# A four-layer graph network in one kernel: the mirrored attention sums leave PSUM through ScalarE and are added in SBUF on GpSimd

## The reference, cut to what matters

```python
h = relu(layernorm(x));  x = x + L0(h, adj)      # (A @ (h @ W + b)) / column degrees
h = relu(layernorm(x));  x = x + L1(h, adj)      # normalised adjacency @ (h @ W), relu
h = relu(layernorm(x));  x = x + L2(h, adj)      # attention, below
h = relu(layernorm(x));  x = x + L3(h, adj)      # hypergraph product with adj

def L2(x, adj, weight, bias):
    h = x @ weight
    h_norm = h / maximum(norm(h, axis=1), 1e-8)
    sim = h_norm @ h_norm.T                       # symmetric
    attn = softmax(sim + log(adj + 1e-8), axis=1) # = (adj + 1e-8) * exp(sim), over its row sum
    return attn @ h + bias
```

## Time and profile before

| what | us |
|---|---|
| median of 3 runs | 1335.18 |
| lowest, highest run | 1329.08, 1477.92 |
| the profiled execution | 1339.48 |
| its span, first to last instruction | 1337.7 |
| attention, first scores to last mirrored product, about | 570 to 1129 |

### The profile page before, as it was taken

The page is one execution under the profiler, slowest core; times in us unless marked ns, Lnnn a source line. Parts: engine busy times, 40 slices in busy tenths (PEclk is TensorE's granted clock), DMA queues, the critical chain, the costliest instruction groups (busy, mean ns, idle before and its releaser), DMA issues.

```text
span 1337.7 us, 26725 instructions
## 1 busy us (share of the span) xinstructions
PE 1271.8 (95%) x9548; PEld 944.0 (71%) x9548; DVE 1012.4 (76%) x2273; ACT 629.6 (47%) x1480; POOL 365.2 (27%) x422
## 2 busy tenths in 40 slices
PE   6999999979999999989999999999999977899998
PEld 4788788854455555557776777777767655688887
DVE  7878789899455555579888978978889988776642
ACT  5654456546223222266656755656656654311111
POOL 2000000012422223213223332332333222465433
PEclk9999999999999999999999999999999999999999
DMA  9999999932111220125653554544544414250500
GB/s 225 247 340 294 307 354 380 382 145 84 48 57 54 63 64 17 48 87 157 198 174 119 174 163 126 173 133 148 177 122 155 135 56 119 79 150 26 150 25 25
DMA packets 122899, 199.93 MB, mean 149 GB/s; under 512 B 13201, under 2 KB 83857, under 8 KB 122769
## 3 DMA queue, kind: packets, MB, share of 16 engines
q1 hardware_dynamic: 115568, 194.04, 47.0%
q10 hardware_dynamic: 7200, 4.20, 1.1%
HBM read 147.85 MB, written 50.33 MB: 148 GB/s over the span
## 4 chain that ended last, share of the span: by engine, by line
PE 55%; issue 13%; DVE 11%; DMA 5%; POOL 4%; ACT 2%; SPq 1%; ACTq 0%; DVEq 0%; POOLq 0%
PE ps L1823 12%; PE ps L1619 8%; PE ps L1620 8%; PE ps L1732 7%; DMA acc<-in_adj 5%; PE ps L1717 5%; PE ps L1718 5%; DVE ring L795 4%; POOL ring L693 3%; PE ps L1784 3%; PE ps L1749 2%; DVE small L807 2%; SPq L431 1%; DVE ring L1043 1%; DVE ring L1073 1%
## 5 line engine op out<-in xcount | busy, mean ns | idle before, releaser
L693 POOL TENSOR_TENSOR ring<-ring 128x512 f16<-128x512 f32 (+3 forms) x133 | 151.9, 1149 | 327.8 <-ACT ring L1493 327.8
L1581 PE MATMUL ps<-val_hi,ring 128*128 128x257 f16 x1024 | 227.2, 274 | 5.0 <-DVE ring L795 5.0
L1582 PE MATMUL ps<-val_lo,ring 128*128 128x256 f16 x1024 | 227.1, 274 | 0.0
L1619 PE MATMUL ps<-ring,acc 128*128 128x512 fp8e4 x512 | 196.7, 384 | 6.7 <-DVE acc L933 6.7
L1732 PE MATMUL ps<-hnt 128*128 128x512 f16 (+3 forms) x864 | 196.3, 363 | 1.0 <-DVE ring L1043 1.0
L1620 PE MATMUL ps<-ring,acc 128*128 128x512 fp8e4 x512 | 196.6, 384 | 0.0
L795 DVE STREAM_TRANSPOSE ring<-acc 128x1024 uint8<-128x1024 uint8 x128 | 151.2, 1219 | 39.1 <-DMA acc<-in_adj 39.0
L1717 PE MATMUL ps<-val_hi,ring 128*128 128x257 f16 x490 | 134.7, 275 | 22.8 <-POOL ring L693 13.9
L1372 ACT ACTIVATE hnt<-ring 128x512 bf16<-128x512 uint8 (+1 forms) x192 | 115.1, 602 | 82.7 <-DVE ring L795 82.7
L1717 PE MATMUL ps<-val_hi,hs 128*128 128x257 f16 x534 | 145.8, 273 | 1.1 <-DVE acc L1106 0.6
L1749 PE MATMUL ps<-val_hi,hs 128*128 128x257 f16 x534 | 145.8, 273 | 0.0
(11 more groups left out here) (234 smaller groups left out, 2371.3 us busy)
## 6 DMA issues: line engine op xcount, KB each, us to landing
acc<-in_adj SPq DMA_DIRECT2D x256, 256.0 KB, 9.3
turned_dram<-ring SPq DMA_DIRECT2D x56, 512.0 KB, 2.9
ring<-turned_dram SPq DMA_DIRECT2D x224, 128.0 KB, 2.9
at_dram<-ring SPq DMA_DIRECT2D x32, 512.0 KB, 9.8
ring<-at_dram SPq DMA_DIRECT2D x64, 256.0 KB, 3.9
ring<-at_dram SPq DMA_DIRECT2D x24, 512.0 KB, 3.8
ring<-at_dram SPq DMA_DIRECT2D x9, 1024.0 KB, 9.7
xs<-in_x SPq DMA_DIRECT2D x12, 256.0 KB, 10.6
```

Of the source, the lines that this page charges most:

```text
L693: nc.gpsimd.tensor_tensor(lo2[m % 2][:, k:GW], p2t[m % 2][:, k:GW], hi2[m % 2][:, k:GW], ALU.subtract).then_inc(sem["lo2_done"], 1)
L1581: nc.tensor.matmul(ps[:, k % 8, 0:D + 1], lhs, val_hi0[:, t, 0:D + 1], start=(t == 0), stop=False)
L1582: last = nc.tensor.matmul(ps[:, k % 8, 0:D], lhs, val_lo0[:, t, :], start=False, stop=(t == NB - 1))
L1619: nc.tensor.matmul(ps[:, bank + c, :], g_hi[:, t, c * P:(c + 1) * P], src, start=(t == 0), stop=False)
```

## The change

The mirrored sum is copied from PSUM by ACT. In group 0 the copy goes straight to the row in `acc`; in later groups it goes to one of two rows of 257 in SBUF (`mirrored`, laid over the bias row and an unused part of the weights), and GpSimd adds it to `acc`. ACT does the copy right behind weights_high, GpSimd the addition ahead of mirror_low. PE's waits for a free bank, and the last layer's first wait, go by the new semaphore acc_copied; acc_added now counts only the 84 additions on GpSimd, and the group sums of DVE and the reuse of a `mirrored` row wait for it. Products, precision and DMAs are as before.

```diff
@@ -35,7 +35,7 @@
...
-s_done exp_raw exp_done turned written p1_done hi1_done lo1_done pv1_done t_done p2_done hi2_done lo2_done pv2_done acc_added
+s_done exp_raw exp_done turned written p1_done hi1_done lo1_done pv1_done t_done p2_done hi2_done lo2_done pv2_done acc_copied acc_added
...
@@ -125,8 +125,8 @@
         p2t = [temps[:, (2 + i) * 1024:(3 + i) * 1024].bitcast(F32) for i in range(2)]
         hi2 = [temps[:, 4096 + i * 512:4608 + i * 512].bitcast(F16) for i in range(2)]
         lo2 = [temps[:, 5120 + i * 512:5632 + i * 512].bitcast(F16) for i in range(2)]
-        w_all = sb("w_all", [P, 3 * C * D], F32)
-        w = w_all[:, :].rearrange("p (l c d) -> p l c d", l=3, c=C)
+        w_all = sb("w_all", [P, 3 * C * D + 1], F32)
+        w = w_all[:, 0:3 * C * D].rearrange("p (l c d) -> p l c d", l=3, c=C)
         w1_hi = w_all[:, 0:256].bitcast(F16).rearrange("p (c d) -> p c d", c=C)
         w1_lo = w_all[:, 256:512].bitcast(F16).rearrange("p (c d) -> p c d", c=C)
         w2_hi = w_all[:, 512:768].bitcast(F16).rearrange("p (c d) -> p c d", c=C)
@@ -134,9 +134,10 @@
         e_t = [ring[:, 6 * N + i * 1024:6 * N + (i + 1) * 1024].bitcast(F32) for i in range(2)]
         turned = [ring[:, a:a + 2048].bitcast(F32) for a in (N + 2048, 6 * N + 2048)]
         back = [ring[:, a:a + 2048].bitcast(F32) for a in (7 * N + 2048, 7 * N)]
-        misc = sb("misc", [P, 3 * D], F32)
+        misc = sb("misc", [P, 3 * D + 1], F32)
         xn = [misc[:, i * D:(i + 1) * D] for i in range(2)]
         bias_bc = misc[:, 2 * D:3 * D]
+        mirrored = [misc[:, 2 * D:3 * D + 1], w_all[:, 5 * D:6 * D + 1]]
         hs = sb("hs", [P, 4 * D], F32)
         ht = [hs[:, i * D:(i + 1) * D] for i in range(2)]
         s32 = [hs[:, (2 + i) * D:(3 + i) * D] for i in range(2)]
@@ -693,6 +694,13 @@
                 nc.gpsimd.tensor_tensor(lo2[m % 2][:, k:GW], p2t[m % 2][:, k:GW], hi2[m % 2][:, k:GW],
                                         ALU.subtract).then_inc(sem["lo2_done"], 1)
 
+            def add_mirror(n):
+
+                (g, j), m = order[n], n_outer[n]
+                pool.wait_ge(sem["acc_copied"], m + 1)
+                since(pool, sem["acc_added"], m - NB + (g + 1) * GB - n_outer[opens[1]])
+                nc.gpsimd.tensor_tensor(acc[:, j, :], acc[:, j, :], mirrored[m % 2], ALU.add).then_inc(sem["acc_added"], 1)
+
             for n in range(NS):
                 if n - 1 in late_at["project1"]:
                     add_bias(late_at["project1"][n - 1])
@@ -700,11 +708,17 @@
                     root_var2(late_at["project1"][n])
                 if n in late_at["project2"]:
                     root_norm(late_at["project2"][n])
+                for o in mirrors_at(n - 1):
+                    if outer[o] and order[o][0] > 0:
+                        add_mirror(o)
                 for o in mirrors_at(n + 1):
                     mirror_low(o)
                 for g, i in tail_at(n):
                     if i == 9:
                         root_var3(g)
+            for o in mirrors_at(NS - 1):
+                if outer[o]:
+                    add_mirror(o)
             root_var3(NG - 2)
             root_var3(NG - 1)
             for n in range(NB // 2):
@@ -1083,16 +1097,6 @@
                                                    ps[:, 6, b0 * P:GW].rearrange("p (b i) -> p b i", i=P),
                                                    ALU.add, ALU.mult).then_inc(sem["p2_done"], 1)
 
-            def add_mirror(n):
-
-                (g, j), m = order[n], n_outer[n]
-                dve.wait_ge(sem["pv2_done"], place[n] + 1)
-                if g == 0:
-                    nc.vector.tensor_copy(acc[:, j, :], ps[:, mirror_bank(n), 0:D + 1]).then_inc(sem["acc_added"], 1)
-                else:
-                    dve.wait_ge(sem["acc_added"], m - NB + (g + 1) * GB)
-                    nc.vector.tensor_tensor(acc[:, j, :], acc[:, j, :], ps[:, mirror_bank(n), 0:D + 1], ALU.add).then_inc(sem["acc_added"], 1)
-
             def group_sum(g, b):
 
                 k = g * GB + b
@@ -1102,7 +1106,8 @@
                 if g == 0:
                     nc.vector.tensor_copy(acc[:, k, :], ps[:, b, 0:D + 1]).then_inc(sem["group_out"], 1)
                 else:
-                    dve.wait_ge(sem["acc_added"], n_outer[opens[g]])
+                    dve.wait_ge(sem["acc_copied"], n_outer[opens[1]])
+                    since(dve, sem["acc_added"], n_outer[opens[g]] - n_outer[opens[1]])
                     nc.vector.tensor_tensor(acc[:, k, :], acc[:, k, :], ps[:, b, 0:D + 1], ALU.add).then_inc(sem["group_out"], 1)
 
             def group_tail(g, i):
@@ -1273,15 +1278,8 @@
                     weights(n + 1)
                 if n + 1 < NS and outer[n + 1]:
                     turn(n + 1)
-                for o in mirrors_at(n - 1):
-                    if outer[o]:
-                        add_mirror(o)
                 if n + 1 < NS:
                     weights_low(n + 1)
-                if n == NS - 1:
-                    for o in mirrors_at(n):
-                        if outer[o]:
-                            add_mirror(o)
                 if n in late_at["transposes_n"]:
                     hnt_low(late_at["transposes_n"][n])
                 if n - 1 in late_at["project1"]:
@@ -1492,6 +1490,18 @@
                 k = mirror_blocks(n)[0] * P
                 nc.scalar.activation(hi2[m % 2][:, k:GW], p2t[m % 2][:, k:GW], ACT.Copy).then_inc(sem["hi2_done"], 1)
 
+            def mirror_out(n):
+
+                m = n_outer[n]
+                act.wait_ge(sem["pv2_done"], place[n] + 1)
+                if order[n][0] == 0:
+                    to = acc[:, order[n][1], :]
+                else:
+                    act.wait_ge(sem["x_biased"], NB)
+                    since(act, sem["acc_added"], m - 1 - n_outer[opens[1]])
+                    to = mirrored[m % 2]
+                nc.scalar.activation(to, ps[:, mirror_bank(n), 0:D + 1], ACT.Copy).then_inc(sem["acc_copied"], 1)
+
             def next_rows(k):
 
 
@@ -1524,6 +1534,9 @@
             for n in range(NS):
                 if n + 1 < NS:
                     weights_high(n + 1)
+                for o in mirrors_at(n - 1):
+                    if outer[o]:
+                        mirror_out(o)
                 if n in late_at["transposes_n"]:
                     hnt_high(late_at["transposes_n"][n])
                 if n in late_at["transposes2"]:
@@ -1764,7 +1780,7 @@
                 pe.wait_ge(sem["exp_done"], n + 1)
                 if n_inner[n] > 0:
                     pe.wait_ge(sem["p2_done"], place[[o for o in range(n) if inner[o]][-1]] + 1)
-                since(pe, sem["acc_added"], sums_in(6, n))
+                since(pe, sem["acc_copied"], sums_in(6, n))
                 for b in mirror_blocks(n):
                     last = nc.tensor.transpose(ps[:, 6, b * P:(b + 1) * P], e_t[n % 2][:, b * P:(b + 1) * P], ident_f[:, :])
                 last.then_inc(sem["t_done"], 1)
@@ -1774,7 +1790,7 @@
                 bank, blocks = (mirror_bank(n), mirror_blocks(n)) if outer[n] else (j % GB, mirror_blocks(n))
                 pe.wait_ge(sem["lo2_done"], m + 1)
                 if outer[n]:
-                    since(pe, sem["acc_added"], sums_in(bank, n))
+                    since(pe, sem["acc_copied"], sums_in(bank, n))
                     if bank == 6:
                         pe.wait_ge(sem["p2_done"], place[max(o for o in range(n) if inner[o])] + 1)
                     if n_outer[n] == 0:
@@ -1852,7 +1868,7 @@
 
             pe.wait_ge(sem["exp_done"], NS)
             pe.wait_ge(sem["p2_done"], NM)
-            pe.wait_ge(sem["acc_added"], n_outer[NS])
+            pe.wait_ge(sem["acc_copied"], n_outer[NS])
             for n in range(3):
                 first_three(n)
                 if n == 2:
```

## The result

The changed kernel takes 1343.13 us (median of 11 runs, 1338.97 to 1358.31), the kernel before 1329.08 us in the same comparison (11 runs, the three shown above among them). The ratio is 1.0153 [1.012, 1.0186]: slower by 1.5%, 16 to 25 us, within the 2%. It leaves the run of 1477.92 us out, and it is not the quotient of the two medians, which lie 14.05 us (1.1%) apart.

A forecast was written before the change was run, and what follows sets the result against it. PE was taken to bound 607 to 1058 us, DVE and its chain 1058 to 1129. Terms of 4.0 + 4.8 + 2.2 + 1.9 = 12.9 us, against the median of 1335.2, gave 1348 us; range 1330 to 1362.

The forecast's parts named there:

- Less the 0.2 that L1050 gains, net 0.33 us: Nearly every pass of groups 1 to 6: the four L1073 pushed back 0.53 us, less L1050's gain of 0.2.
- The 0.53 of the earlier trace: At 616.11 us a GpSimd addition meets four L1073, which take 1.42 us instead of 0.89; taken for each meeting.
- starts of groups 2 to 5: Four group starts: delays of 1.39 us each, less 0.4 of cover, leave 1.0; together 4.0 us.
- behind the tails, groups 1 to 4: Steps 9 to 13: five additions of 0.33 make 1.65 us, less 0.45 of cover; four times, 4.8 us.
- end of group 5, start of group 6: From 1058 to 1094 us, without cover: two additions of 0.33 and three of 0.53 make 2.2 us.
- group 7: Before the last mirrored products: two additions of 0.53 make 1.1 us.
- last addition, to L1174: End of the attention: the last addition ends 0.8 us later, passing through to PE's wait in the last layer.
- a cover of 0.4 to 0.45: Group starts and steps 9 to 13: delay taken as absorbed, chosen between none and DVE's normal wait of 0.54 us.
- The bank's hand-over: In late passes ScalarE's copy frees the PSUM bank 0.6 us later; taken as 0, upper end 3.0 us.
- the lock blocks in full: Rival, 17%: every contended addition costs 0.72 us rather than 0.53; together 20.2 us, giving 1355.
- No cover: Rival, 12%: 48 additions each cost the full 0.53 us and the banks count; 29.2 us, giving 1364.
- DVE's relief wins: Rival, 24%: DVE's time only shrinks, 5.0 us in late passes, less 0.8 at the end; 1331.

The follow-up runs named there:

- e1: The changed kernel, but GpSimd adds only the first of the 257 columns, with every wait and copy kept; 1324.84 us, ratio to before 1.0001.
- f1: The changed kernel, but two GpSimd memsets, which read nothing from SBUF, replace each addition; 1329.83 us, ratio to before 1.0009.
- f4: The changed kernel with a second GpSimd addition, of the side row to itself, behind each first one; 1378.76 us, ratio to before 1.0379.
- g1: The kernel before, with VectorE's own addition in groups 1 to 7 cut to one of 257 columns; 1326.15 us, ratio to before 0.9953.
- f2: The changed kernel, but GpSimd adds only 128 of the 257 columns; 1338.35 us, ratio to before 1.0067.
- e2: The changed kernel, but VectorE instead of ScalarE copies the sum out of PSUM, and GpSimd still adds; 1342.69 us, ratio to before 1.0117.
- e4: The changed kernel with ScalarE's copy ahead of weights_high in the second to fourth passes of groups 1 to 7 and two late passes; 1343.41 us, ratio 1.0144.
- g2: The changed kernel with ScalarE's copy ahead of weights_high only in the second to fourth passes of groups 1 to 5; 1344.33 us, ratio to before 1.0127.

## Why the prediction was right or wrong

Forecast 1348, measured 1343.13; the sum was +12.9 us, the ratio gives about +20 and the matched stretches 17.7 + 0.75 = 18.4. That the total came within 5 us is partly luck: the sum was 5.5 us short of the matched stretches, and the median of three runs that it was added to, 1335.18, was 6.1 us above the median of eleven, 1329.08.

**Right: the cause.** The lock on two SBUF inputs, its meeting with L1087 and its place behind ScalarE's copy were as forecast. e1 and f1 show it: with less read by GpSimd, or nothing, the loss is gone. The Trainium skill (SBUF — State Buffer, section on the two separate sides) has this exclusion, and for VectorE instructions with two SBUF inputs it has it only against GpSimd instructions that read SBUF. These runs agree: beside a memset of 0.31 us the four take 0.88 us, beside the addition 1.33 to 1.43.

**Right: what costs nothing.** ScalarE's copy without the full addition (e1: 558.7), and the middle of the groups: from step 18 to a group's end and from 6 to 9 the difference is 0.00 us. f4 shows the limit of that cover.

**Wrong: the size of one pass's delay, and the cover.** "Less the 0.2 that L1050 gains, net 0.33 us" is the first step that failed. The time from the start of `weights` to the end of `mirror_weights` in one pass, medians of the 9 to 13 full-width passes that start between 744 and 792 us, read from the rows of DVE in the traces:

| kernel | that time | `weights_low` | the four |
|---|---|---|---|
| before | 3.10 | 0.69 | 0.89 |
| g1, relief alone | 3.00 | 0.81 | 0.88 |
| f1, memsets | 3.01 | 0.81 | 0.88 |
| f2, 128 columns | 3.26 | 0.81 | 1.12 |
| after | 3.78 | 1.15 | 1.38 (1.33 and 1.42 by turns) |
| f4, two additions | 4.20 | 1.15 | 1.80 (1.75 and 1.84 by turns) |

The 0.53 of the earlier trace rows for the four is met in every other pass (1.42 against 0.89), in the rest it is 0.44. But net it is 0.68, not 0.33. I counted one meeting in each pass and here there are two: the four end later, so ScalarE's rounding and `mirror_low` start later, 0.82 us after `weights` instead of 0.49, and most of `mirror_low` falls on `weights_low`, 0.46 us more. The four's 0.44 or 0.53 and this 0.46, less the 0.2 by which `weights_low` begins earlier (as forecast: 1.38 us after `weights` instead of 1.57), make 0.70 or 0.79; 0.68 and 0.77 are measured by turns. The second meeting comes mostly where VectorE is late and begins the pass without a wait: `weights_low` takes over 0.75 us in 30 of the 92 full-width passes of groups 1 to 7, before in 6. The trace of before shows one of these 6:

```profile
758.31 1.16 POOL L693 TENSOR_TENSOR ring<-ring 128x512 f16<-128x512 f32 x1 [2.10 <-ACT ring L1493]
759.03 0.98 DVE L1050 SCALAR_TENSOR_TENSOR hs<-ring,hs 128x512 f16<-128x512 f32 x1
```

L1050, issued while `mirror_low` runs to 759.47, takes 0.98 us instead of 0.69. The forecast did not use this row. Of the relief of 0.2 only 0.1 is left even in g1, where `weights_low`, starting earlier, waits 0.12 us for `mirror_low`.

**What it made of the terms**, from the start of every third step's scores in both traces:

| term | predicted | measured |
|---|---|---|
| starts of groups 2 to 5 | 4.0 | 7.6 |
| behind the tails, groups 1 to 4 | 4.8 | 6.7 |
| end of group 5, start of group 6 | 2.2 | 2.2 |
| group 7 | 1.1 | 1.0 |
| last addition, to L1174 | 0.8 | 0.75 |

The other 0.2 us lie in group 1. The last three terms stand; there the cover was taken as none. The two where I chose a cover of 0.4 to 0.45 are the ones that fell short, and that choice is the second step that failed. Without it the same counts give 1.39 for a start and 1.65 behind a tail; measured are 1.52 to 1.55 (steps 3 to 6) and 1.4 to 1.8. The sum with no cover is 16.3 us, most of the way to 18.4. Another 1.4 us lie in the first three steps of groups 4 and 5, which no term had. The second term also lay later than forecast, at steps 12 to 18: DVE's step without waiting is 3.80 us, so a late DVE gains 0.13 a step on PE's 3.93, where it gained 0.54 before, and it stays late through more steps. The cover itself had shrunk with the change. How much of the shortfall is the second meeting and how much the cover was not measured singly.

**The bank's hand-over**, held at 0 with 3.0 as upper end: PE does wait 20.0 us on it, but e2, with the same additions and no ScalarE in it, takes 576.3. That it costs nothing of its own holds there. But e4 and g2, which free the bank earlier, shorten the starts by 0.9 us and keep 1.7 of the 8.5 us of groups 1 to 3; so at the starts it is part of the path, which I had not counted.

**The rivals.** The size is nearest to "the lock blocks in full" (20.2), and its mechanism is borne out, though not its price. Whichever comes second waits for all that is left of the other's instruction: L1064 ends 0.55 us after `mirror_low`, the addition 0.59 after L1064, the first L1087 0.15 after the addition (rows of the normal step). But the addition takes 0.64 us by itself and not 0.72, the four are issued just before its turn begins, and so a meeting costs them 0.44 to 0.53; the rest of the size is the second meeting. "No cover" (29.2) was right in the missing cover, but its price of the full 0.53 for each of 48 additions and 3.0 us for the banks is far above the 18.4 measured. "DVE's relief wins" forecast -4.2 without the lock; g1 and f1, which come nearest to that case, gain 3.2 and 1.7. Its size was about right and its condition false. Of the signs named, L1073 by some 40 us (33.6) and the wait for L1169 near 1.8 (1.36) came somewhat short, GpSimd's 60 or more (79.2) came; PE's waits named in the earlier trace rows grew by 12.7 us, but for the bank: that for `mirror_low` went from 13.9 to 15.2 us, not up by 8 to 12. (PE's idle time in the earlier trace rows is 6.7 + 18.3 = 25.0 us, not 24.9; nothing hangs on it.)
